# Layer norms by pairs of batches, three pairs of four normalised on ScalarE, and three stores of the result

## The reference

```
x = _layernorm(x + _L0_attn_ref(x, ...))
x = _layernorm(x + _L0_xattn_ref(ctx_2048, ctx_2048, x, ...))
x = _layernorm(x + _L0_ffn_ref(x, ...))
x = _layernorm(x + _L1_attn_ref(x, ...))
x = _layernorm(x + _L1_xattn_ref(x, ..., ctx_2048, ctx_2048, 8))
x = _layernorm(x + _L1_ffn_ref(x, ...))

def _layernorm(x, axis=-1, eps=1e-05):
    m = jnp.mean(x, axis=axis, keepdims=True)
    v = jnp.var(x, axis=axis, keepdims=True)
    return (x - m) / jnp.sqrt(v + eps)
```

## Time and profile before

| | us |
|---|---|
| median of 3 runs | 1034.2 (1031.79 to 1034.71) |
| profiled execution, its own time | 1035.04 |
| span of the profiled execution | 1033.2 |
| busy: PE, DVE, ACT, POOL | 932.0, 688.7, 390.6, 277.9 |
| first addition of norms 0 to 5 | 244.83, 316.70, 559.96, 759.80, 832.81, 1021.01 |
| granted clock of TensorE, mean | 0.953 |

### The profile page before, as it was taken

One profiled execution on the slowest core, in us unless ns is written; L12 is line 12 of the kernel. 1 busy time (PEld: TensorE's weight loads), 2 busy tenths in 40 slices (PEclk: granted clock), 3 DMA queues, 4 the chain that ended last, 5 costly groups with the idle time before them and its releaser, 6 DMA issues. The chain is left out here.

```text
span 1033.2 us, 15019 instructions
## 1 busy us (share of the span) xinstructions
PE 932.0 (90%) x4792; PEld 701.9 (68%) x4792; DVE 688.7 (67%) x1225; ACT 390.6 (38%) x863; POOL 277.9 (27%) x262
## 2 busy tenths in 40 slices
PE   5999999996876799999997979999979869999995
PEld 4788888885335688888886758888863347555554
DVE  3666666667997645544456578889758988555553
ACT  2555555555003233323323215555540035454441
POOL 3122221111660112222222053324028723144200
PEclk9999999998995899999999889999989979999998
DMA  7101111110103111111112000000001012111000
GB/s 262 40 23 41 41 41 41 41 48 9 40 22 77 30 39 40 44 46 46 46 50 94 1 1 1 1 0 1 2 0 36 25 42 89 49 54 54 1 1 41
DMA packets 21752, 40.17 MB, mean 39 GB/s; under 512 B 2544, under 2 KB 13552, under 8 KB 20464
## 3 DMA queue, kind: packets, MB, share of 16 engines
q1 hardware_dynamic: 21712, 39.66, 12.1%
HBM read 38.60 MB, written 1.05 MB: 38 GB/s over the span
## 5 line engine op out<-in xcount | busy, mean ns | idle before, releaser
L1295 PE MATMUL bank<-xTh,ringh 128*128 128x512 f32 x432 | 176.5, 409 | 12.3 <-DVE xTl L853 11.4
L1296 PE MATMUL bank<-xTl,ringh 128*128 128x512 f32 x432 | 173.4, 401 | 0.0
L1297 PE MATMUL bank<-xTh,ringl 128*128 128x512 f32 x432 | 172.5, 399 | 0.0
L1295 PEld LDWEIGHTS bank<-xTh,ringh 128*128 128x128 f32 x432 | 83.1, 192 | 29.1 <-DVE xTl L853 11.4
L1297 PEld LDWEIGHTS bank<-xTh,ringl 128*128 128x128 f32 x432 | 82.5, 191 | 20.1
L1296 PEld LDWEIGHTS bank<-xTl,ringh 128*128 128x128 f32 x432 | 83.2, 193 | 15.3
L831 ACT ACTIVATE SF<-bank 128x512 f32<-128x512 f32 x108 | 62.7, 597 | 70.2 <-PE bank L1638 40.4
L1272 DVE TENSOR_TENSOR HF<-bank,SF 128x512 f32<-128x512 f32 x96 | 64.5, 690 | 36.4 <-PE bank L1638 29.9
L1072 DVE TENSOR_TENSOR arena<-bank,arena 128x512 f32<-128x512 f32 x48 | 33.2, 691 | 72.9 <-PE bank L1297 72.9
L777 ACT ACTIVATE Eh<-arena 128x512 fp32r<-128x512 f32 x48 | 30.3, 632 | 115.4 <-DVE arena L1076 115.4
L1638 PE MATMUL bank<-astk,bstk 128*128 128x512 f32 x192 | 67.1, 444 | 5.5 <-DVE HF L1272 3.3
(11 more groups left out here) (228 smaller groups left out, 2197.3 us busy)
## 6 DMA issues: line engine op xcount, KB each, us to landing
ring<-w_attn SPq DMA_DIRECT2D x16, 384.0 KB, 3.2
ring<-w_moe SPq DMA_DIRECT2D x24, 256.0 KB, 2.7
lowraw<-w_low SPq DMA_DIRECT2D x6, 1024.0 KB, 5.9
toep<-toep SPq DMA_DIRECT2D x32, 128.0 KB, 2.1
outring<-w_down SPq DMA_DIRECT2D x24, 128.0 KB, 2.0
outring<-wo_attn SPq DMA_DIRECT2D x16, 128.0 KB, 2.0
ring<-w_ffn SPq DMA_DIRECT2D x6, 256.0 KB, 5.2
wq<-w_attn SPq DMA_DIRECT2D x1, 1344.0 KB, 13.6
```

Source lines behind the costliest of these rows:

```text
L1295: pe.matmul(o, ringh[:, slot, wc], xTh[:, k, halves[j]], start=(k == 0), stop=False)
L1296: pe.matmul(o, ringh[:, slot, wc], xTl[:, k, halves[j]], start=False, stop=False)
L1297: ins = pe.matmul(o, ringl[:, slot, wc], xTh[:, k, halves[j]], start=False, stop=(k == DK - 1))
```

## The change

Each norm goes by pairs of batches. VectorE adds one bank, takes the statistics of its two batches, and goes on to the next pair's addition while ScalarE takes the square root. `rstd` of a pair follows behind the next pair's addition. `shift` is formed by one SCALAR_TENSOR_TENSOR (line 958 of the changed kernel) straight from the mean and `rstd`, so that `nmean` goes. ScalarE normalises pairs 0, 1 and 2, and VectorE only pair 3. TensorE's waits name the new counts. The result leaves in three stores: four batches, two batches, two batches.

```
-                add(2 * lead)
-                link(add(2 * lead + 1))
-                statistics(lead)
-                add(2 - 2 * lead)
-                link(add(3 - 2 * lead))
-                deviation_inverse(lead)
-                dve.tensor_tensor(shift[:], nmean[:], rstd[:, 4 * lead:4 * lead + 4], ALU.mult).then_inc(ln_scale, 1)
-                statistics(1 - lead)
-                deviation_inverse(1 - lead)
-                for b in range(4 - 4 * lead, B - 4 * lead):
+                order = (2 * lead, 2 * lead + 1, 2 - 2 * lead, 3 - 2 * lead)
+                def variance(i):
+                    for b in range(pair(i).start, pair(i).stop):
+                        ins = dve.bn_stats(st[:, b, :], rN[:, b, :])
+                    link(ins)
+                    for b in range(pair(i).start, pair(i).stop):
+                        ins = dve.bn_aggr(mv[:, b, :], st[:, b, :])
+                    link(ins)
+                    dve.tensor_scalar(ve[:, pair(i)], mv[:, pair(i), 1], EPS, None, ALU.add).then_inc(ln_var, 1)
+                def scale(i):
+                    dve.wait_ge(ln_sd, 4 * layer_norm + i + 1)
+                    link(dve.reciprocal(rstd[:, pair(i)], sd[:, pair(i)]))
+                    if i < 3:
+                        dve.scalar_tensor_tensor(shift[:, pair(i)], mv[:, pair(i), 0], -1.0, rstd[:, pair(i)],
+                                                 ALU.mult, ALU.mult).then_inc(ln_scale, 1)
+                add(0)
+                variance(0)
+                for i in range(1, 4):
+                    add(i)
+                    scale(i - 1)
+                    variance(i)
+                scale(3)
+                for b in range(pair(3).start, pair(3).stop):
                     dve.tensor_scalar(xN[:, b, :], rN[:, b, :], mv[:, b, 0:1], rstd[:, b:b + 1],
                                       ALU.subtract, ALU.mult).then_inc(ln_x1, 1)
...
-                deviations(lead)
-                act.wait_ge(ln_scale, layer_norm + 1)
-                for i in range(B // 2):
-                    b = lead * B // 2 + i
-                    act.activation(xN[:, b, :], rN[:, b, :], ACT.Identity, bias=shift[:, i:i + 1],
-                                   scale=rstd[:, b:b + 1]).then_inc(ln_x0, 1)
-                deviations(1 - lead)
+                deviation(0)
+                for i, q in enumerate(order[:3]):
+                    act.wait_ge(ln_scale, 3 * layer_norm + i + 1)
+                    for b in (2 * q, 2 * q + 1):
+                        act.activation(xN[:, b, :], rN[:, b, :], ACT.Identity, bias=shift[:, b:b + 1],
+                                       scale=rstd[:, b:b + 1]).then_inc(ln_x0, 1)
+                    deviation(i + 1)
...
-                    pe.wait_ge(ln_x1 if b >= 4 else ln_x0, 4 * layer_norm + b % 4 + 1)
+                    if b < 6:
+                        pe.wait_ge(ln_x0, 6 * layer_norm + b + 1)
+                    else:
+                        pe.wait_ge(ln_x1, 2 * layer_norm + b - 5)
...
-            for j, done in ((1, ln_x0), (0, ln_x1)):
-                sp.wait_ge(done, 6 * B // 2)
+            for part, done, n in ((slice(4, 8), ln_x0, 34), (slice(0, 2), ln_x0, 36), (slice(2, 4), ln_x1, 12)):
+                sp.wait_ge(done, n)
+                sp.dma_start(out[:, part, :], xN[:, part, :]).then_inc(out_done, 16)
```

More of the change, by code:

```diff
@@ L129, in decoder_layers @@
         rstd = sb("rstd", [P, B])
-        nmean = sb("nmean", [P, B // 2])
-        shift = sb("shift", [P, B // 2])
+        shift = sb("shift", [P, B])
         ident = cst[:, C_ID:C_ID + P]
@@ L480, in _ @@
                 load_ffn1(f, f % 2)
-            for j, done in ((1, ln_x0), (0, ln_x1)):
-                sp.wait_ge(done, 6 * B // 2)
-                half = slice(j * B // 2, (j + 1) * B // 2)
-                sp.dma_start(out[:, half, :], xN[:, half, :]).then_inc(out_done, 16)
-            sp.wait_ge(out_done, 32)
+            for part, done, n in ((slice(4, 8), ln_x0, 34), (slice(0, 2), ln_x0, 36), (slice(2, 4), ln_x1, 12)):
+                sp.wait_ge(done, n)
+                sp.dma_start(out[:, part, :], xN[:, part, :]).then_inc(out_done, 16)
+            sp.wait_ge(out_done, 48)
         @block.gpsimd
@@ L733, in norm_and_turn, with deviation @@
             def norm_and_turn(layer_norm, turn=True, high=False, lead=0):
[L735 to L738, removed]
-                deviations(lead)
-                act.wait_ge(ln_scale, layer_norm + 1)
-                for i in range(B // 2):
-                    b = lead * B // 2 + i
-                    act.activation(xN[:, b, :], rN[:, b, :], ACT.Identity, bias=shift[:, i:i + 1],
-                                   scale=rstd[:, b:b + 1]).then_inc(ln_x0, 1)
-                deviations(1 - lead)
+                order = (2 * lead, 2 * lead + 1, 2 - 2 * lead, 3 - 2 * lead)
+                def deviation(i):
+                    two = slice(2 * order[i], 2 * order[i] + 2)
+                    act.wait_ge(ln_var, 4 * layer_norm + i + 1)
+                    act.activation(sd[:, two], ve[:, two], ACT.Sqrt).then_inc(ln_sd, 1)
+                deviation(0)
[5 more added lines that the diff above has]
+                    deviation(i + 1)
                 if not turn:
@@ L931, in norm @@
                 if layer_norm > 0:
[L932 to L941, removed]
+                    dve.wait_ge(ln_x0, 6 * layer_norm)
@@ new lines, in norm, with pair, add @@
+                order = (2 * lead, 2 * lead + 1, 2 - 2 * lead, 3 - 2 * lead)
+                def pair(i):
+                    return slice(2 * order[i], 2 * order[i] + 2)
+                def add(i):
+                    dve.wait_ge(produced, steps[order[i]])
+                    link(dve.tensor_tensor(rN[:, pair(i), :],
+                                           bank[:, first_bank + order[i], :].rearrange("p (b d) -> p b d", b=2),
+                                           xN[:, pair(i), :], ALU.add))
@@ L942, in statistics @@
+                def variance(i):
+                    for b in range(pair(i).start, pair(i).stop):
                         ins = dve.bn_stats(st[:, b, :], rN[:, b, :])
                     link(ins)
-                    for b in range(4 * j, 4 * j + 4):
+                    for b in range(pair(i).start, pair(i).stop):
                         ins = dve.bn_aggr(mv[:, b, :], st[:, b, :])
                     link(ins)
-                    half = slice(4 * j, 4 * j + 4)
-                    dve.tensor_scalar(ve[:, half], mv[:, half, 1], EPS, None, ALU.add).then_inc(ln_var, 1)
```

## The result

| | before | changed | ratio |
|---|---|---|---|
| median | 1032.97 us of 20 (1031.00 to 1034.94) | 1035.71 us of 20 (1034.72 to 1037.94) | 1.0027, interval 1.0019 to 1.0035 |
| profiled execution, its span | 1035.04, 1033.2 | 1036.69, 1034.7 | |
| granted clock, mean | 0.953 | 0.945 | |

The change costs 2.7 us, 0.27%. The forecast was 5.1 us more than before. The sign was right, and the size about half of what was forecast. The absolute 1035.7 lies inside the predicted range, but partly because the kernel before came out 1.2 us lower in more executions.

What follows compares the result with a forecast made beforehand. TensorE, busy 90% of the span, waits at six norms, so their chains counted. Terms 1.5 + 2.3 + 0.3 + 0 + 0.1 + 0.9 = +5.1 us gave 1039.3 us on the runs' median; range 1034.5 to 1043.5.

Steps and rivals of the forecast that it cites:

- The sign: Whole kernel: the change makes it slower, by 5.1 us; slower by over 0.3% was given 0.71.
- The chain: VectorE in an undisturbed norm: 2.15 us a pair from pair 1 on, last normalisation ending at 9.61 us, 0.44 later.
- Norms 1 and 4: Norms without GpSimd: ScalarE's first copy starts at 8.76 us instead of 8.01, +0.75 each, +1.5 us.
- 0.13 behind the root: ScalarE's first copy: starts 0.13 us behind the fourth root, the time an already met wait costs, so at 8.76.
- Norm 2: Norm beside GpSimd: stalled `shift` and `ve` make the copies start at 571.7 instead of 569.20; +2.3 us in all.
- The catches: Norm 2: `shift` of pair 0, `ve` and `shift` of pair 1 wait for GpSimd, 1.4, 1.2 and 0.5 us.
- Norm 3: An earlier front, but GpSimd stalls `ve` and `shift` of pair 2, 2.8 us against 1.7; third copy later, +0.3 us.
- Norm 0: Front gains 1.05 us; GpSimd may catch `shift` of pair 0 and `ve` of pair 1; taken as 0 (-0.6 to +0.45).
- Norm 5: Last norm: last normalisation +0.43 us, smaller last store saves 0.3, together +0.1.
- The clock: TensorE's clock may rise late behind norms 0 and 4, 1.8 us a norm, 3.6 for both; taken as 0.9.
- Nothing is caught: Rival for norms beside GpSimd: no instruction waits, the early start pays, -2.2 us, 1032.0; chance 0.12.
- Small terms cancel: Rival: norm 0 at its lower end, fewer catches in norm 2, no clock term; +1 to +2, 1035.7; chance 0.13.

Runs made afterwards that it cites:

- e2: The changed kernel with GpSimd held out of norms 0, 2 and 3 until the norm's last normalisation; 1037.37 us, one execution.
- e6: The changed kernel without `ve` (epsilon as the root's bias), with `shift` as two one-column tensor_scalar instructions; 1029.53 us, ratio 0.9967 to the kernel before.
- e3: The kernel before with only its result in three stores (four batches, two, two); 1033.43 us, ratio 1.0004.
- e10: The kernel before with `nmean` and `shift` packed in one buffer, so later buffers lie as in the changed kernel; 1033.07 us, ratio 0.9988.
- e9: The changed kernel with an unused buffer where `nmean` stood, so later buffers lie as in the kernel before; 1040.5 us, ratio 1.0077.
- e5: The changed kernel with ScalarE normalising only pairs 0 and 1 and VectorE pairs 2 and 3; 1039.2 us, ratio 1.0062 to the kernel before.
- e1: The kernel before with GpSimd held out of norms 0, 2 and 3 until the norm's last normalisation; 1036.99 us, one execution.
- e8: The changed kernel without `ve`, with unused TensorE products ahead of each pair's transposes and behind the last; 1021.88 us, ratio 0.9889 to the kernel before.
- e4: The changed kernel without `ve`, the square root taking epsilon as its bias; 1029.35 us, ratio 0.9958 to the kernel before.
- e7: The kernel before with unused TensorE products only ahead of each norm's first transposes; 1033.43 us, ratio 1.0004.

## Why the prediction was right or wrong

**The chain, right.** The pair of 2.15 us and its place in the norm came out within 0.03 us. The fused `shift`, which had no row, took 0.16 as assumed, in norm 4 above and in all norms of e2. One reading of the kernel before was wrong without harm: VectorE is not without a gap there, it waits 0.30 us for the second root ahead of the reciprocal at 840.38, and the sum for the new chain does count such a wait.

**Norms 1 and 4, mis-sized.** Forecast +0.75 each, measured +0.40 and +0.48. The term that was mis-sized is the start of the copies, "0.13 behind the root". ScalarE started the copy 0.11 us behind the *start* of the 0.20 us root (840.14 to 840.25), so at 8.52 and not 8.76.

**Norm 2, right but smaller.** The catches were those forecast. +2.3 became +1.94, for the same 0.24 at the copies' start. The rule of the Trainium skill that was weighed here ("SBUF — State Buffer", "Who interferes with whom") holds for `ve` and the fused `shift`. e6's one-column tensor_scalar with a pointer scalar was not caught (two of them in 0.33 us).

**Norm 3, right:** +0.3, measured +0.26, with the two catches in place.

**Norm 0.** Taken as 0, measured +0.08 against the profiled execution before. But e3 and e10, whose norm 0 is the kernel before's, took 11.87 and 11.88, so beside them it is +0.9. The two catches of the changed kernel are not the two that were foreseen:

```profile
245.69 0.70 DVE L952 TENSOR_SCALAR ve<-mv 128x2 f32<-128x2 f32 x1
...
248.36 1.02 DVE L952 TENSOR_SCALAR ve<-mv 128x2 f32<-128x2 f32 x1
```

GpSimd started 0.8 us behind pair 0's `shift` and met `ve` of pairs 1 and 2. In e9 it met `shift` of pair 0 and `ve` of pair 1. Where the catch falls turns on tenths of a microsecond.

**Norm 5, right in both terms.** Last normalisation +0.40 (forecast 0.43), smaller store -0.2 (forecast 0.3), so +0.2 in place of +0.1.

**The clock, mis-sized.** Forecast 0.9. Behind norm 4 the clock rose to 2.4 GHz at 848.8, 5.6 us into the next stage, where it had been up at that stage's start:

```profile
843.20:850.00 6.80, 6.80 (x18) 5.39 (x19) 6.41 (x9) 2.97 (x6) 3.73 (x6) 0.58 0.39 145
```

```profile
843.80:850.60 6.80, 6.48 (x31) 5.04 (x31) 6.34 (x9) 3.61 (x6) 4.93 (x7) 1.00 0.38 113
```

(the changed kernel, then the kernel before: 18 products against 31 in the same time, and the first product takes 0.77 us at 843.16). The stage grew by 1.87 us, as that place of the prediction priced it (1.8). Counted from the norm's first addition the clock rose at 14.9 to 17.2 us in the changed kernel, e2, e5 and e9. In the kernel before and e3 it rose at 10.5 to 10.6. But in e1 and e10, which have the old order, it rose at 14.2 to 14.7. So the pairs make the late rise usual, and the halves don't exclude it. The mean granted clock points the same way: 0.943 to 0.946 in all 20 executions of the changed kernel, 0.949 to 0.954 in all those of the kernel before that were timed beside the experiments. Behind norm 0 there is no such term: there the late rise, 1.9 us too, is the usual case for both orders (e3 60.95), and the profiled execution of the kernel before was the exception (59.18). I had read that one execution as the rule.

**The step that failed: the buffer's place was put at nothing, -2.6 us.** I costed the removal of `nmean` as an instruction only. As a buffer it shifted the addresses behind it, and the expert blocks and attention heads, which the change doesn't name, became shorter (e9, e10). This is what took the result below the forecast and brought it within 0.3% of the kernel before. By the profiled executions the norms gave +3.4 (forecast 4.2), the clock +1.9 (forecast 0.9), together 5.3 where 5.1 was forecast, and the layout -2.6: +2.7, as measured. So two wrong sizes in the forecast nearly cancelled, and the missing term is the miss.

That the sum closes so well is in part luck. The clock's 1.9 is the difference of one execution of each kernel, and with norm 0 counted against e3 and e10 the sum is +3.5, 0.8 above the measured difference. And the runs that switch the layout don't give 2.6 for the whole kernel: with the addresses of before the change costs 7.0 us (e9, against the kernel before), with the new addresses in both kernels 3 to 4 (the changed kernel against e10, each by its distance from the kernel before). The blocks and heads are shown for each layout; the 2.6 as a share of the total is a sum over them.

**The rivals.** "Nothing is caught" fell with the first stretched row. "Small terms cancel" named 1035.7, the measured time, but not for its reasons: the small terms did not cancel each other, the layout made up for them.

**Left open.** Why 32 bytes matter to the matmuls. The operands of the blocks' gate and up products (`xTh`, `xTl`, the weight ring) did not move; `lowraw` and all that lies behind it did, `arena`, `Eh` and `El` among it, and with them the operands of the down products. Yet about 0.05 of the 0.066 us of a block lies in the gate and up products: one on `xTh` and `ringh` is followed by the next after 234 ns in the kernel before and e9, and after 232 in the changed kernel and e10. So it is not the matmul's own operands alone. No run moved one buffer alone. Open too is why e10 gained less as a whole than its blocks.

## What to carry to other kernels

Before you call a finer grain cheaper, count its chained instructions. Here the pairs added two reciprocals, two `shift`s and two `ve`s a norm, and removing all `ve`s was worth 6.4 us, more than the whole change cost. When a buffer is dropped or resized, treat the new addresses as a part of the change, and test it with a pad of the same size. Do not read a term of a microsecond or two from one execution where the clock's rise differs from one execution to the next: see it in a second one first.

## What the runs showed of the hardware

- Dropping `nmean` and widening `shift`, which moved the buffers behind them (by 32 bytes a partition, as inferred), changed an expert block from 8.933 to 8.867 us and an attention head from 13.97 to 13.91. The last feed-forward did not follow (its products on `astk` spanned 127.15 and 127.01 us in the kernel before and e9, 127.01 and 127.10 in the changed kernel and e10).
- VectorE beside GpSimd: a fused `shift` of two columns waited up to 1.70 us, `ve` up to 1.46, while a tensor_scalar of one column (two in 0.33 us), the reciprocal, statistics and aggregation kept their times.
- Unused products on TensorE won 7.5 us where they filled the pauses ahead of, between and behind the transposes (e8 against e4), and nothing where they stood only ahead of the first ones (e7).
- On ScalarE a copy that waited for nothing else started 0.11 us behind the start of a 0.20 us root, in the changed kernel and in e5.
